# A mixture-of-experts tail: order of the weight splits, place of the result additions, and the last three program pieces made one

## The reference, cut to what matters

```python
h = layernorm(x) @ W_in + b_in                 # 2048 tokens of 256
probs = softmax(h @ W_gate + b_gate)           # 8 experts
topv, topi = top_k(probs, 2); topv = topv / topv.sum(-1)
route = zeros_like(probs) with topv at topi
mid  = relu(h @ W1[e] + b1[e])                 # 256 -> 1024, per expert
eout = mid @ W2[e] + b2[e]                     # 1024 -> 256
moe  = sum over e of route[n, e] * eout[n, e]
out  = x + moe @ W_out + b_out
```

## Time and profile before

| | us |
|---|---|
| median of 3 runs | 1544.39 (1540.24 to 1544.46) |
| the profiled execution | 1542.99 |
| its span | 1541.2 |

### The profile page before, as it was taken

One profiled execution on the slowest core, in us unless ns is written; L12 is line 12 of the kernel. 1 busy time (PEld: TensorE's weight loads), 2 busy tenths in 40 slices (PEclk: granted clock), 3 DMA queues, 4 the chain that ended last, 5 costly groups with the idle time before them and its releaser, 6 DMA issues. The chain is left out here.

```text
span 1541.2 us, 27459 instructions
## 1 busy us (share of the span) xinstructions
PE 1313.6 (85%) x9627; PEld 1034.4 (67%) x9627; DVE 1020.0 (66%) x2009; ACT 872.4 (57%) x2183; POOL 471.3 (31%) x626
## 2 busy tenths in 40 slices
PE   5989999997899999878998666899663999999975
PEld 3534444355799999767887444788552988889973
DVE  5788787634465665457668976788546677777743
ACT  5336666763656656442222664788433777777743
POOL 5313222254333434231002654111103244444420
PEclk9979999997999999989998875999975999999997
DMA  3835352000000000030002100222024666666725
GB/s 85 227 61 149 50 74 46 2 4 28 1 2 1 2 1 1 1 116 0 1 1 69 23 1 21 48 51 49 12 66 134 189 207 208 215 205 204 215 80 164
DMA packets 97964, 116.28 MB, mean 75 GB/s; under 512 B 23469, under 2 KB 83235, under 8 KB 97827
## 3 DMA queue, kind: packets, MB, share of 16 engines
q1 hardware_dynamic: 88403, 99.96, 24.6%
q0 software_dynamic: 4416, 12.06, 2.2%
q10 hardware_dynamic: 5008, 2.49, 0.7%
HBM read 88.61 MB, written 16.55 MB: 68 GB/s over the span
## 5 line engine op out<-in xcount | busy, mean ns | idle before, releaser
L827 ACT ACTIVATE sa_probs<-ps 128x512 f32<-128x512 f32 (+1 forms) x304 | 154.4, 579 | 86.1 <-PE ps L780 85.0
L851 DVE TENSOR_REDUCE sa_top<-ps 128x2 f32<-128x1024 f32 (+3 forms) x160 | 171.9, 1115 | 39.1 <-PE ps L756 25.3
L2489 PE MATMUL ps<-me_h,me_w_parts 128*128 128x256 f32 x1104 | 141.9, 289 | 18.4 <-issue 16.9
L2489 PEld LDWEIGHTS ps<-me_h,me_w_parts 128*128 128x128 f32 x1104 | 137.1, 193 | 23.1 <-issue 20.1
L3043 ACT ACTIVATE room<-ps,cx_top 128x154 f32<-128x154 f32 x256 | 97.0, 388 | 89.8 <-DVE cx_top L3107 89.8
L2503 PE MATMUL ps<-me_w_parts,me_mid 128*128 128x256 f32 x1104 | 136.3, 283 | 5.8 <-DVE me_result L2583 5.6
L2503 PEld LDWEIGHTS ps<-me_w_parts,me_mid 128*128 128x128 f32 x1104 | 132.3, 188 | 9.8 <-issue 9.7
L2553 ACT ACTIVATE me_full<-ps,me_b 128x256 f32<-128x256 f32 x184 | 94.6, 514 | 70.0 <-PE ps L2489 66.9
L2566 DVE TENSOR_TENSOR me_w_parts<-me_chunk,me_w_parts 128x1024 fp32r<-128x1024 f32 x92 | 118.1, 1284 | 17.1 <-ACT me_w_parts L2530 14.7
L2595 DVE TENSOR_TENSOR me_mid<-me_full,me_mid 128x256 fp32r<-128x256 f32 x184 | 84.3, 462 | 67.0 <-ACT me_mid L2555 62.0
L2905 POOL TENSOR_TENSOR room<-room 128x512 f32<-128x512 f32 x64 | 66.7, 1042 | 173.6 <-DVE room L3115 173.5
(11 more groups left out here) (456 smaller groups left out, 3433.1 us busy)
## 6 DMA issues: line engine op xcount, KB each, us to landing
me_chunk<-in_L_ffn_W_dram SPq DMA_DIRECT2D x92, 512.0 KB, 5.3
sa_k<-scr_k SPq DMA_DIRECT2D x48, 128.0 KB, 4.5
sa_q<-scr_q SPq DMA_DIRECT2D x96, 64.0 KB, 4.4
cn_qd<-cn_qh SPq DMA_DIRECT2D x60, 64.0 KB, 2.0
scr_q<-room SPq DMA_DIRECT2D x6, 512.0 KB, 4.9
scr_k<-room SPq DMA_DIRECT2D x6, 512.0 KB, 5.3
me_b<-in_L_ffn_b_dram SPq DMA_DIRECT2D x23, 128.0 KB, 4.6
x<-in_x_dram SPq DMA_DIRECT2D x4, 512.0 KB, 6.2
```

What stands on the lines that cost most here:

```text
L827: act.activation(probs[:, step % self.PROBS, h0:h0 + many, 0:w], src[:, :, 0:w], ACT.Exp, scale=DH ** -0.5).then_inc(exped.sem, 1)
L851: dve.tensor_reduce(top2[:, k % 2, k0 // 512, h0:h0 + many, sb % HBLK], src[:, :, 0:w], AX.X, ALU.max).then_inc(freed.sem, 1)
L2489: last = pe.matmul(ps[:, MID + n % 4, 0:RT], w[:, u % 2, 0, i, DM * k + P * b:DM * k + P * b + P], h[:, u % 2, j, k, :], start=(m == 0), s ...
```

## The change

1. Chunks get new numbers (`chunk_at`): after the first two come the first-layer chunks of tile u+1, then the second-layer chunks of tile u, and so on. `SPLITS` puts the first-layer splits of tile u+1 after blocks 2 and 5, and both second-layer splits of tile u after block 7. SyncE loads in the same new order, and the biases of tile u+1 go between them.
2. `finish(u - 2)` comes after block 1. The scatter of each half tile waits for its own addition alone.
3. Expert, collecting and storing piece are one block. SyncE and ScalarE wait for all scatters themselves, VectorE for GpSimd's bias additions. The loads come in groups of 1, 1, 2, 4, 4 and 4 token tiles, the stores in groups of 4, 4, 4, 2, 1 and 1, each as soon as its tiles are added. The buffers of the collecting part are views of those of the experts. The arithmetic is the same.

```diff
+class Collect:
+    GROUPS = ((0, 1), (1, 1), (2, 2), (4, 4), (8, 4), (12, 4))
+    STORES = ((0, 4), (4, 4), (8, 4), (12, 2), (14, 1), (15, 1))
...
+    def load(self, eng, j):
+        for g, (t, n) in enumerate(self.GROUPS):
+            r0 = N * j + P * t
+            eng.dma_start(self.got[:, j, t:t + n, :], self.results[r0:r0 + n * P, :].rearrange("(t p) d -> p t d", p=P)
+                          ).then_inc(self.got_in[j][g].sem, 16)
...
+    def store(self, sp):
+        for t, n in self.STORES:
+            sp.wait_ge(self.added.sem, self.added.at(t + n))
+            sp.dma_start(self.out_rows.rearrange("b (t p) d -> p (b t) d", p=P)[:, t:t + n, :], self.c.x[:, t:t + n, :]
+                         ).then_inc(self.sent.sem, 16)
+        sp.wait_ge(self.sent.sem, self.sent.at(16 * len(self.STORES)))
...
+    # tensor(), scalar(), vector(): the bodies of moe_collect, vector() with this ahead
+        dve.wait_ge(self.biased.sem, self.biased.at(NT))
...
+        collect = Collect(c, results, out_rows, share, w_out, raw(w[:, :, :, :, :]), row, full, biased)
-        SPLITS = {2: (2,), 5: (3,), HB - 2: (4,), HB - 1: (5,)}
+        SPLITS = {2: (0,), 5: (1,), HB - 1: (2, 3)}
+        def chunk_at(layer, u, q):
+            if layer == 0:
+                return q if u == 0 else 4 * u - 2 + q
+            return min(4 * u + 4, 4 * TILES - 2) + q
...
+        def scattered(eng):
+            for i in range(2):
+                eng.wait_ge(stored[i].sem, stored[i].at(16 * SUB * len(range(i, TILES, 2))))
...
-                for u in range(TILES):
-                    e = sp.value_load(pr.expert[0:1, u:u + 1], min_val=0, max_val=E8 - 1)
...
-                    weights(0)
-                    weights(1)
                     if u >= BUF:
                         sp.wait_ge(added.sem, added.at(SUB * (u - BUF + 1)))
...
-                    weights(2)
-                    weights(3)
+                e = expert(0)
+                weights(0, 0, e, 0)
+                weights(0, 0, e, 1)
+                biases(0, e)
+                for u in range(TILES):
+                    if u + 1 < TILES:
+                        after = expert(u + 1)
+                        weights(0, u + 1, after, 0)
+                        weights(0, u + 1, after, 1)
+                        biases(u + 1, after)
+                    weights(1, u, e, 0)
+                    weights(1, u, e, 1)
+                    e = after
+                scattered(sp)
+                collect.load(sp, 0)
+                collect.store(sp)
...
                 def scatter(u):
-                    pool.wait_ge(added.sem, added.at(SUB * (u + 1)))
                     for a in range(SUB):
+                        pool.wait_ge(added.sem, added.at(SUB * u + a + 1))
...
                 scatter(TILES - 1)
-                pool.wait_ge(biased.sem, biased.at(NT))
-                for i in range(2):
-                    pool.wait_ge(stored[i].sem, stored[i].at(16 * SUB * len(range(i, TILES, 2))))
...
                 def first(u):
-                    pe.wait_ge(w_low.sem, w_low.at(4 * u + 2))
+                    pe.wait_ge(w_low.sem, w_low.at(chunk_at(0, u, 1) + 1))
...
                 def second(u):
-                    pe.wait_ge(w_low.sem, w_low.at(4 * u + 4))
+                    pe.wait_ge(w_low.sem, w_low.at(chunk_at(1, u, 1) + 1))
...
+                scattered(act)
+                collect.load(act, 1)
+                collect.scalar(act)
...
-                        if b == 4 and u >= 2:
+                        if b == 1 and u >= 2:
                             finish(u - 2)
```

More of the change, by code:

```diff
@@ L2406, in _, with expert, weights, biases @@
                 pr.sync_stores(sp, tokens, b1_cols)
-                for u in range(TILES):
-                    e = sp.value_load(pr.expert[0:1, u:u + 1], min_val=0, max_val=E8 - 1)
[L2410 to L2423, removed]
-                    weights(0)
-                    weights(1)
+                def expert(u):
+                    return sp.value_load(pr.expert[0:1, u:u + 1], min_val=0, max_val=E8 - 1)
+                def weights(layer, u, e, q):
+                    n = chunk_at(layer, u, q)
+                    if n >= BUF:
+                        sp.wait_ge(w_low.sem, w_low.at(n - BUF + 1))
+                    if layer == 0:
+                        src = c.arg["L1_ffn_W1"][bass.ds(e, 1), P * q:P * q + P, :].rearrange("a p n -> p (a n)")
+                        dst = chunk[:, n % BUF, :]
+                    else:
+                        r0 = DM // 2 * q
+                        src = c.arg["L1_ffn_W2"][bass.ds(e, 1), r0:r0 + DM // 2, :].rearrange("a (k p) n -> p (a k) n", p=P)
+                        dst = chunk[:, n % BUF, :].rearrange("p (k n) -> p k n", n=D)
+                    sp.dma_start(dst, src).then_inc(w_in[n % BUF].sem, 16)
+                def biases(u, e):
                     if u >= BUF:
@@ L2517, in _ @@
                     second(u)
+                collect.tensor(pe)
             @block.scalar
@@ L2521, in split @@
                 def split(n):
-                    u, q = divmod(n, 4)
+                    layer, u, q = owner[n]
                     act.wait_ge(w_in[n % BUF].sem, w_in[n % BUF].at(16 * (n // BUF + 1)))
-                    if u >= 2 and q < 2:
+                    if u >= 2 and layer == 0:
                         act.wait_ge(mm.sem, mm.at(HB * (u - 1)))
@@ L2604, in _ @@
                 finish(TILES - 1)
+                collect.vector(dve)
         pr.done()
+        collect.done()
         for i in range(BUF):
@@ L2612, in moe_experts @@
             s.passed(k)
[L2615 to L2698, removed]
-        for s, k in ((weighed, NT), (summed, NT), (turned, NT), (copied, NT), (mm, NT), (added, NT)):
-            s.passed(k)
@@ L2703, in store @@
-def store(c, out):
-    nc = c.nc
-    sent = c.sig("stored")
-    with nc.Block() as block:
-        @block.sync
-        def _(sp):
-            for b in range(4):
-                sp.dma_start(out.rearrange("b (t p) d -> p (b t) d", p=P)[:, 4 * b:4 * b + 4, :],
-                                      c.x[:, 4 * b:4 * b + 4, :]).then_inc(sent.sem, 16)
-            sp.wait_ge(sent.sem, sent.at(64))
 def build(nc, arg, out):
@@ L2730, in build @@
             c.new_stage()
-        moe(c, scratch)
-        store(c, out)
+        moe(c, scratch, out)
 def self_wide_cross_ffn(c, ct, scratch, far):
```

88 lines of the change are left out of this document (81 added, 7 removed).

## The result

The changed kernel takes 1495.72 us (median of 4 runs, 1492.49 to 1497.92) against 1544.24 us before (4 runs): ratio 0.969, 95% interval 0.9674 to 0.9706. The profiled execution has a span of 1494.0 us against 1541.2.

What follows compares the result with a forecast made beforehand. TensorE was taken to bound the expert stage, apart from small stalls. Savings of 21.8 (expert stage and start), 8.8 (scatters to load), 2.5 (first load) and 5.0 (end) sum to 38.1 us: 1505.5 us predicted, range 1499 to 1517.

Steps and rivals of the forecast that it cites:

- 12.61 - 0.27 = 12.34 us is what the matmuls alone need: Expert stage: TensorE's tile period falls to 12.34 us once its stalls go, saving 18.3 us over 20 periods.
- the early additions: Expert stage: result additions at block 1 remove TensorE's 0.27 us wait before the second layer of each tile.
- that move: GpSimd's 1.74 us bias addition moves from VectorE's blocks 6 and 7 to 4 and 5; slack covers it, cost nothing.
- The timing inside a tile: From first(u)'s start: additions near +3.1 us, late splits from +9.1, VectorE's take at +10.3, 2 us before TensorE is ready.
- SyncE's queue: Bias loads waiting for additions of tile u-2 delay two second-layer chunks, issued +5.0 and +5.5 us; priced at nothing.
- B: Rival: the ring through additions, SyncE's loads and splits closes at 12.9 us a tile, 11 us back, 1517; chance 0.10.
- D: Rival: same ring at SyncE's bias wait with 9.3 us landings, period 14.8, 49 us back, 1554, slower; chance 0.04.
- Last scatters to first load: Between experts and collecting: first load 3.6 instead of 12.44 us after the last result addition starts, saving 8.8 (7.8 to 9.8).
- the 8.5 us: Gap without bytes or instructions before the first collecting load: taken as block closing; rival A, scatters' completion, 1513, chance 0.10.
- The end: Stores following the tiles leave one 128 KB store, 3.3 instead of 8.3 us after the last addition, saving 5.0 (3 to 5.6).
- The start: first(1) begins 2.4 us earlier as the take comes sooner; the 0.43 us stall before first(2) goes too.
- later groups are ahead: Collecting part: load groups after the first stay ahead of TensorE's pace, 256 KB moving in 0.75 us against 1.1 a tile.

Runs made afterwards that it cites:

- e1: Changed kernel with the result additions moved back from after block 1 to after block 4: 1512.8 us, ratio 0.9799 to the kernel before.
- e2: Changed kernel with the result additions moved from after block 1 to after block 5: 1577.05 us, ratio 1.0218 to the kernel before.
- e3: Kernel before with only the result additions moved from after block 4 to after block 1: 1527.03 us, ratio 0.9888.
- e7: Kernel before with GpSimd's bias addition done on only 1 of 256 columns: 1533.7 us, ratio 0.9932.
- e4: Kernel before with GpSimd not draining its DMA queue at the end of the expert piece: 1535.14 us, ratio 0.9953.
- e6: Changed kernel plus idle matmuls, 24 before first(1) and 56 before the collecting part: 1493.48 us, ratio 0.9692 to the kernel before.
- a1_again: The changed kernel run again unaltered, beside two versions with idle matmuls: 1497.79 us, ratio 0.9721 to the kernel before.

## Why the prediction was wrong, and where it was right

The direction was right, and so were the places of the stalls and of the gaps in the sum. What failed is the price of the stalls: the floor that TensorE's period was to fall to, and with it the view of what set the old period. (1505.5 was also a little off my own sum: 1504.9 and the 1.4 us of the median make 1506.3.)

**The step that failed** is "12.61 - 0.27 = 12.34 us is what the matmuls alone need". It is 11.94, and 246.8 - 238.95 is 7.9 of the 9 us by which the sum was short. It had two faults, and the runs show both. First, an idle time in a row is counted from the modelled end of the matmuls before, but without a wait the second layer starts 0.24 us ahead of that end; a wait there costs its idle time and those 0.24 us (e1, e2). Second, the period from which I subtracted was not TensorE's. In it VectorE's last split ends 0.1 us before first(22) starts, so it was the chain's 12.62 (e3, e7), in which TensorE's 0.27 cost nothing at all. VectorE's timeline of the kernel before:

```profile
1473.69 1.23 DVE L2566 TENSOR_TENSOR me_w_parts<-me_chunk,me_w_parts 128x1024 fp32r<-128x1024 f32 x1
```

The first fault is 0.24 of the 0.40 us, the second the other 0.16: with the same wait of 0.27 us but without that chain, e1 has 12.45 instead of 12.61. The middle tile could have warned me, since 13.42 - 0.74 - 0.27 is 12.41 and not 12.34. The floor stood in the old trace, in stretches with no wait at either end. TensorE's timeline of the kernel before:

```profile
1203.23 0.60 PE L2476 MATMUL ps<-ident,me_row 128*128 128x128 f32 x4
1203.59 5.93 PE L2503 MATMUL ps<-me_w_parts,me_mid 128*128 128x256 f32 x48
...
1430.74 5.93 PE L2503 MATMUL ps<-me_w_parts,me_mid 128*128 128x256 f32 x48
1436.51 5.96 PE L2489 MATMUL ps<-me_h,me_w_parts 128*128 128x256 f32 x48
...
1449.87 5.95 PE L2489 MATMUL ps<-me_h,me_w_parts 128*128 128x256 f32 x48
1455.66 0.60 PE L2476 MATMUL ps<-ident,me_row 128*128 128x128 f32 x4
```

0.36 + 5.77 + 5.79 = 11.92 us, start to start: a sum of pieces would have given 26.7 us for the 20 periods, where 26.1 were saved.

**What gave the 26 us.** I gave the early additions the smaller part, 0.27 us a tile. Alone they are worth 0.8 (e3), not through the wait but through what they take along: the scatters, and behind them GpSimd's bias addition, which no longer falls on VectorE's last splits. I had priced that move at nothing. In the new order no cost of it shows, with the take done 1.9 us before first(u+1); in the old period it was worth 0.8.

**The timing inside a tile** held: additions at first(u) + 2.97 us (3.1 forecast), take done on VectorE at + 10.0 (10.3), late splits from + 9.06 (9.1). VectorE and ScalarE in the middle tile of the kernel after:

```profile
1329.32 0.75 DVE L2715 TENSOR_TENSOR me_result<-ps,me_b 128x256 f32<-128x256 f32 x2
...
1333.84 1.21 DVE L2698 TENSOR_TENSOR me_w_parts<-me_chunk,me_w_parts 128x1024 fp32r<-128x1024 f32 x1
...
1335.67 0.69 DVE L2703 TENSOR_TENSOR me_h<-ps,me_h 128x512 fp32r<-128x512 f32 x1
```

```profile
1335.41 2.12 ACT L2659 ACTIVATE me_w_parts<-me_chunk 128x1024 fp32r<-128x1024 f32 x2
```

**SyncE's queue** (rivals B and D) was read wrongly in its place, not in its wait. The bias loads of tile v wait for the additions of tile v-4, in both kernels (the description ahead of the prediction says v-3). But SyncE is a tile further ahead than I reckoned: during first(u) it issues the bias loads of tile u+2, so they do wait for the additions of tile u-2. It reaches them late. The chunk ahead of them waits for VectorE's split after block 5, until 1333.84 + 1.21 = 1335.05, and by then those additions have been done for 5 us (1329.32 + 0.75). So the additions hold back nothing, and no ring closes through them. The first bias load and, below it, the landing of the chunks in the kernel after:

```profile
1335.86 0.23 SPq L2544 DMA_DIRECT2D me_b<-moe_b  x1
...
DMA to landing us min/median/max: 3.7/4.1/5.6
```

It is issued 9.5 us into the tile, not 3.95, and no chunk is late: 3.7 to 5.6 us against 4.8 to 6.6. The price of nothing was right, by luck.

**Last scatters to first load** was right: 3.13 us against 3.6, within the bounds. What was argued of the 8.5 us is now shown by e4. The last scatter's instruction ends at 1464.72 (1463.75 + 0.97), the load is issued at 1466.18, and the DMA view shows bytes moving until about 1465.7, some 0.5 us before that (slots of 0.1 us from 1463 on):

```profile
GB/s 0 0 0 0 0 0 0 0 0 0 0 0 0 0 0 0 0 0 0 0 0 0 41 492 369 328 82 0 0 0 0 0 0 0 0 0 0 0 0 0
```

By the Trainium skill, "DMA: Bandwidth & Descriptors", section "Anatomy of one DMA — SWDGE (gpsimd) path", most of a fixed 2 us is the write receipt, which would have put the load later still; the measured 0.5 us decides.

**The end** was better than forecast (2.4 instead of 3.3 us from the end of the last addition to the span's end). **The start** was worse by 1 us: first(1) did begin 2.4 us earlier after first(0), but lasted 8.58 instead of 7.44 us at a granted clock of 0.66 against 0.78. A shorter idle time before it (3.66 us) did not keep the clock, and why it was lower than before is not shown; matmuls in the gap did keep it (e6). **The collecting part**: "later groups are ahead" failed. The 256 KB loads, third in their queues, landed after 5.0 and 5.8 us, and ScalarE waited 0.48 us for rows of the third tile. In a1_again, the same kernel, they landed after 6.7 and 6.9 us, ScalarE waited 2.03 us, and the part took 23.6 us; so the price is not the same in every execution.

## What to carry to other kernels

Take the floor of a loop from start-to-start distances of stretches without a wait, piece by piece, never from a period less the idle times in its rows; and before subtracting a stall, ask whether its engine sets that period at all. When work moves, follow what hangs behind it on other engines: here the bias addition two steps behind the result additions was worth more than the wait that they ended. Where a program piece ends after indirect DMAs of GpSimd, its drain is worth a look.

## What the runs showed of the hardware

A drain of GpSimd's DMA queue at the end of a piece costs 7.6 us after the last scatter has been waited for (12.44 against 4.83 us), and nothing that is seen when other work runs beside it. A wait of TensorE costs more than the idle shown, since matmuls that do not wait start before the modelled end of those ahead: 0.24 us more before the second layer, at 0.27 and at 2.67 us of idle alike (e1, e2), and 0.16 before the first layer (e3). After 2.67 us of idle the second layer ran at a lower granted clock in 13 of 20 tiles, for 1.5 us more in 12 of them (e2). GpSimd's bias addition and VectorE's split and block part slow each other when they fall together: 1.74 us against 0.93 on GpSimd, 1.59 and 0.95 against 1.21 and 0.42 on VectorE.
